# A recurrent attention loop rescheduled: compact softmax factors, shared vector passes, attention moved by transfers

## The reference

```python
Pn = rmsnorm(P, input_norm_w)              # context: 4 x 64 x 256
k_proj = Pn @ Wk.T
v_proj = Pn @ Wv.T
for _ in range(NUM_ITERS):                 # 3
    sn = rmsnorm(slots, slot_norm_w)       # slots: 4 x 1024 x 256
    q_proj = sn @ Wq.T
    scores = jnp.einsum('bkd,bmd->bkm', q_proj, k_proj) * SCALE
    attn = jax.nn.softmax(scores, axis=-2)             # over the 1024 slots
    attn = attn / (jnp.sum(attn, axis=-1, keepdims=True) + EPS)   # over the 64 context rows
    updates = jnp.einsum('bkm,bmd->bkd', attn, v_proj)
    slots = gru_cell(updates, slots, gru_wih, gru_whh, gru_bih, gru_bhh)
...
# gru_cell: r = sigmoid(xr + hr); z = sigmoid(xz + hz); n = tanh(xn + r * hn)
#           new = (1 - z) * n + z * h
...
x = x + tanh(g_xattn) * slots
x = x + tanh(g_ffn) * moe(layernorm(x))    # 16 experts, and a shared one
```

## Time and profile before

| | us |
|---|---|
| median of 3 runs | 1268.45 (1265.12 to 1269.66) |
| profiled execution | 1267.16 |
| its span, first to last instruction | 1265.4 |
| loop, TensorE's first to last unit | 92.9 to 457.6 |
| experts and dense part after it | 462.7 to the end |

### The profile page before, as it was taken

The page is one execution under the profiler, slowest core; times in us unless marked ns, Lnnn a source line. Parts: engine busy times, 40 slices in busy tenths (PEclk is TensorE's granted clock), DMA queues, the critical chain, the costliest instruction groups (busy, mean ns, idle before and its releaser), DMA issues. The chain is left out here.

```text
span 1265.4 us, 18034 instructions
## 1 busy us (share of the span) xinstructions
PE 1140.1 (90%) x6000; PEld 952.3 (75%) x6000; DVE 880.7 (70%) x1618; ACT 567.6 (45%) x834; POOL 414.0 (33%) x319
## 2 busy tenths in 40 slices
PE   5659989898999864799997999999999999999995
PEld 3447767676777654688886888888888888888884
DVE  7586787878788669677894566666666666666652
ACT  4244545454545426423223544545454455454441
POOL 4242333333310024234353143334332343332331
PEclk9659999999999986899998999999999999999998
DMA  4200000000000034400014444444444444444421
GB/s 153 89 9 9 1 17 1 17 0 17 0 17 9 9 118 133 125 17 33 17 34 150 154 118 125 129 134 112 106 125 126 134 134 114 103 129 120 134 35 17
DMA packets 45603, 95.58 MB, mean 76 GB/s; under 512 B 11008, under 2 KB 36864, under 8 KB 41216
## 3 DMA queue, kind: packets, MB, share of 16 engines
q1 hardware_dynamic: 31808, 75.98, 18.1%
q0 software_dynamic: 12288, 17.31, 8.2%
q10 hardware_dynamic: 1472, 1.84, 0.4%
HBM read 74.11 MB, written 17.07 MB: 72 GB/s over the span
## 5 line engine op out<-in xcount | busy, mean ns | idle before, releaser
L1921 DVE SCALAR_TENSOR_TENSOR ehid<-eup,b_up,esilu 128x512 f32<-128x512 f32 x128 | 96.1, 751 | 180.9 <-PE eup L1790 164.7
L1758 POOL DMA_INDIRECT out_tokens<-yo,idx_out x64 | 114.9, 1796 | 240.5 <-DVE yo L1895 225.9
L1844 ACT ACTIVATE esilu<-egate,b_gate 128x512 f32<-128x512 f32 x128 | 87.7, 685 | 156.6 <-PE egate L1790 153.5
L1803 PE MATMUL edown<-w_hi,eh_hi 128*128 128x256 f32 x512 | 145.3, 284 | 0.0
L1803 PE MATMUL edown<-w_hi,eh_lo 128*128 128x256 f32 x512 | 144.3, 282 | 0.0
L1803 PE MATMUL edown<-w_lo,eh_hi 128*128 128x256 f32 x512 | 143.0, 279 | 0.0
L1853 ACT ACTIVATE eh_hi<-ehid 128x512 fp32r<-128x512 f32 x128 | 81.1, 633 | 114.9 <-DVE ehid L1921 114.9
L1873 DVE TENSOR_TENSOR w_lo<-raw,w_hi 128x768 fp32r<-128x768 f32 x128 | 121.2, 949 | 2.0 <-ACT w_hi L1833 2.0
L522 PE MATMUL gate_banks<-slots_hi,whh_hi 128*128 128x512 f32 x288 | 117.4, 408 | 4.6 <-ACT tr L660 4.5
L522 PE MATMUL gate_banks<-slots_hi,whh_lo 128*128 128x512 f32 x288 | 114.7, 398 | 0.0
L522 PE MATMUL gate_banks<-slots_lo,whh_hi 128*128 128x512 f32 x288 | 114.6, 398 | 0.0
(11 more groups left out here) (287 smaller groups left out, 2698.9 us busy)
## 6 DMA issues: line engine op xcount, KB each, us to landing
raw<-in_w_expert SPq DMA_DIRECT2D x32, 1536.0 KB
token_rows<-work SPq DMA_DIRECT2D x8, 512.0 KB, 3.2
out_tokens<-y SPq DMA_DIRECT2D x8, 512.0 KB, 3.0
attn<-attn_lo SPq DMA_DIRECT2D x24, 128.0 KB, 2.3
work<-in_x SPq DMA_DIRECT2D x4, 512.0 KB, 4.8
raw<-in_x SPq DMA_DIRECT2D x4, 512.0 KB, 6.7
b_down<-in_down_b SPq DMA_DIRECT2D x1, 2048.0 KB, 9.2
raw<-in_w_shared SPq DMA_DIRECT2D x1, 1536.0 KB, 11.3
```

The costliest lines, as they stand in the source:

```text
L1758: pool.indirect_dma_start(out, bass.IndirectOffsetOnAxis(idx_out[:, j:j + 1], 0), yo[:, j, :], None, compute_op=ALU.add).then_inc(g_add, 16)
L1803: last = nc.tensor.matmul(edown[:, j // 2, (j % 2) * D:(j % 2 + 1) * D], h[:, f % RING, tok], w[:, f, 4 * P:6 * P], start=(f == 0 and m == ...
L1844: nc.scalar.activation(esilu[:, f % 2, :], egate[:, f % 2, :], ACT.Silu, bias=b_gate[:, bass.ds(e, 1), f:f + 1].rearrange("p a b -> p (a b ...
L1921: nc.vector.scalar_tensor_tensor(ehid[:, f % 2, :], eup[:, f % 2, :], b_up[:, bass.ds(e, 1), f:f + 1].rearrange("p a b -> p (a b)"), esilu ...
```

## The change

It leaves setup's results, the number of matmuls for gates and scores, the dense part and the experts as they are. In the loop:

- **Column sums and their reciprocal in compact form.** `column_sums` makes a 128 x 16 tile (tokens on partitions; eight matmuls with `expo` as the weights and a 128 x 2 `rsum` as the moving operand). VectorE adds epsilon and takes the reciprocal there, and splits it in a high and a low part (`two_parts`, in `rec_parts`). `turn_rec` transposes it, `own_columns` lays it out in `spread`, `spread_rec` spreads it over the partitions into the `score` bank. `copy_csum` and the wide reciprocals are gone. `rms` is split in the same way, and both spreads are fp32r matmuls over 128 rows in place of fp32 ones over 16.
- **Placement.** `turn_rms` stands right behind `scores`; `spread_rms` in and behind unit (1,0); `column_sums` in unit (2,0), `turn_rec` behind it, `spread_rec` in unit (2,1). VectorE does `token_rms` and `spread_steps` ahead of the slot passes of group 0, scaling and `maximum` between the two `pre` of group 1, attention in group 2 and its low part in group 3.
- **Shared vector passes.** The three passes that make new slots run once per group over both chunks (1024 columns) instead of once per unit. `tz` is doubled for this.
- **Attention by transfers.** `attention_hi` writes the high part into `rms_c`, `attention_lo` the low part in place into `expo`, each over 128 rows in one instruction; `move_attention` brings both to `attn` with four transfers for each half instead of two.
- **GpSimd** keeps squares, sums and low parts, now released by group (`v_new`). It has three memsets more at the start of the loop, and four selections more in setup.

```diff
                 def column_sums(s):
 
                     pe.wait_ge(v_rsum, s + 1)
+                    for c in range(2 * BLK):
+                        last = nc.tensor.matmul(csum_t.rearrange("p (b c) -> p b c", b=2)[:, :, c],
+                                                expo[:, c * P:(c + 1) * P], rsum[:, :], start=True, stop=True)
+                    last.then_inc(m_csum, 1)
+
+                def turn_rec(s):
+
+                    pe.wait_ge(v_recd, s + 1)
+                    nc.tensor.transpose(rms_b[:, 0:P], rec_parts[:, :], ident[:, :]).then_inc(m_rect, 1)
+
+                def spread_rec(s):
+
+                    pe.wait_ge(v_dia2, s + 1)
                     for h in range(2):
-                        nc.tensor.matmul(score[:, h, :], rsum[:, :], expo[:, h * GROUP:(h + 1) * GROUP],
-                                         start=True, stop=True).then_inc(m_csum, 1)
+                        nc.tensor.matmul(score[:, h, :], pick_group[:, h, :], spread[:, :, :].rearrange("p b t -> p (b t)"),
+                                         start=True, stop=True).then_inc(m_rec, 1)
...
                         sum_squares(pe, first_run - 1, 1 - pair, GPP - 1, (v_ms, s))
                         scores(s, 1 - pair, first_run - GPP)
-                    gru_unit(it, pair, 1, 0, (lambda: turn_rms(s)) if softmax else None)
-                    if softmax:
-                        spread_rms(s, 0)
-                    gru_unit(it, pair, 1, 1)
+                        turn_rms(s)
+                    gru_unit(it, pair, 1, 0, (lambda: spread_rms(s, 0)) if softmax else None)
                     if softmax:
                         spread_rms(s, 1)
+                    gru_unit(it, pair, 1, 1)
                     if more:
                         sum_squares(pe, first_run, pair, 0, (v_ms, s + 1))
-                    gru_unit(it, pair, 2, 0)
-                    gru_unit(it, pair, 2, 1)
+                    gru_unit(it, pair, 2, 0, (lambda: column_sums(s)) if softmax else None)
                     if softmax:
-                        column_sums(s)
+                        turn_rec(s)
+                    gru_unit(it, pair, 2, 1, (lambda: spread_rec(s)) if softmax else None)
...
-                def move_low(s, pair, h):
-
+                def move_attention(s, pair, h):
+
+                    half = slice(h * GROUP, (h + 1) * GROUP)
                     sp.wait_ge(v_alo, 2 * s + h + 1)
                     for b in range(2):
-                        sp.dma_start(attn[rows_of(1 - b), pair, b, h * GROUP:(h + 1) * GROUP].bitcast(F32),
-                                     attn_lo[rows_of(b), :].bitcast(F32)).then_inc(d_alo, 16)
+                        sp.dma_start(attn[rows_of(b), pair, b, half].bitcast(F32), rms_c[rows_of(b), h, :]).then_inc(d_attn[h], 16)
+                        sp.dma_start(attn[rows_of(1 - b), pair, b, half].bitcast(F32), expo[rows_of(b), half]).then_inc(d_attn[h], 16)
...
+                    gru_unit(it, pair, 0, 0, None, (last_high,) if softmax else ())
+                    gru_unit(it, pair, 0, 1)
+                    if softmax:
+                        gru_unit(it, pair, 1, 0, lambda: copy_rms(s, 0), high(0), (lambda: copy_rms(s, 1),))
+                        gru_unit(it, pair, 1, 1, None, (lambda: exponentials(s),))
                     else:
...
+                        gru_unit(it, pair, 1, 0, None, high(0))
+                        gru_unit(it, pair, 1, 1)
+                    gru_unit(it, pair, 2, 0, None, high(1))
+                    gru_unit(it, pair, 2, 1, None, tuple((lambda h=h: attention_hi(s, h)) for h in range(2)) if softmax else ())
+                    gru_unit(it, pair, 3, 0, None, high(2))
                     gru_unit(it, pair, 3, 1)
...
-                def gru_unit(it, pair, g4, c, meanwhile=None):
-
-
-                    u = it * UNITS + (pair * GPP + g4) * 2 + c
+                def gru_group(it, pair, g4, first=(), second=()):
+
+
+                    g = it * G + pair * GPP + g4
                     sl = tokens(pair, g4)
...
+                    for c, between in enumerate((first, second)):
+                        u = it * UNITS + (pair * GPP + g4) * 2 + c
+                        dve.wait_ge(a_r, u + 2)
+                        dve.wait_ge(a_h, u + 2)
+                        nc.vector.scalar_tensor_tensor(pre[:, :], tr[:, c, :], 1.0, hb[:, c, :], ALU.add,
+                                                       ALU.mult).then_inc(v_q, 1)
+                        dve.wait_ge(v_q, u + 3)
+                        dve.wait_ge(m_x, u + 1)
+                        nc.vector.tensor_tensor(pre[:, :], pre[:, :], gate_x[:, :], ALU.add).then_inc(v_pre, 1)
+                        for step in between:
+                            step()
                     dve.wait_ge(a_n, u + 1)
-                    nc.vector.tensor_tensor(dif[:, :], slots[:, c, sl], nn[:, c, :], ALU.subtract).then_inc(v_dif, 1)
-                    dve.wait_ge(v_dif, u + 1)
+                    nc.vector.tensor_tensor(dif[:, :, :], slots[:, :, sl], nn[:, :, :], ALU.subtract).then_inc(v_mix, 1)
+                    dve.wait_ge(v_mix, 2 * g + 1)
                     dve.wait_ge(a_z, u + 2)
...
+                def two_parts(parts, full, v_high, count, v_done):
+
+                    high, low = parts[:, 0:NB].bitcast(F32R), parts[:, LOW:NR].bitcast(F32R)
+                    nc.vector.tensor_copy(high, full[:, :]).then_inc(v_high, 1)
+                    dve.wait_ge(v_high, count)
+                    nc.vector.tensor_tensor(low, full[:, :], parts[:, 0:NB], ALU.subtract).then_inc(v_done, 1)
...
+                def csum_reciprocal(s):
+
+                    dve.wait_ge(m_csum, s + 1)
+                    nc.vector.tensor_scalar(csum_e[:, :], csum_t, ATTN_EPS, None, ALU.add).then_inc(v_rec, 1)
+                    dve.wait_ge(v_rec, 3 * s + 1)
+                    nc.vector.reciprocal(rec[:, :], csum_e[:, :]).then_inc(v_rec, 1)
+                    dve.wait_ge(v_rec, 3 * s + 2)
+                    two_parts(rec_parts, rec, v_rec, 3 * (s + 1), v_recd)
...
+                    gru_group(it, pair, 0, (), (lambda: token_rms(s, 1 - pair), lambda: spread_steps(s)))
+                    gru_group(it, pair, 1, (lambda: scale_scores(s, 0), lambda: scale_scores(s, 1), lambda: maximum(s)),
+                              (lambda: token_sum(s),))
+                    csum_reciprocal(s)
+                    gru_group(it, pair, 2, (lambda: spread_reciprocal(s), lambda: attention_half(s, 0),
+                                            lambda: attention_half(s, 1)))
+                    gru_group(it, pair, 3, (lambda: attention_lo(s, 0), lambda: attention_lo(s, 1)))
```

More of the change, by code:

```diff
@@ L451, in flamingo_kernel @@
             v_q = sem("v_q")
-            v_pre, v_dif, v_mix, v_new = (sem(f"v_{n}") for n in ("pre", "dif", "mix", "new"))
+            v_pre, v_mix, v_new = (sem(f"v_{n}") for n in ("pre", "mix", "new"))
             v_ms = sem("v_ms")
@@ L561, in gru_unit, with scores @@
                     from_attention(gate_x, 4 + c, True).then_inc(m_x, 1)
-                def scores(s, pair, split_before):
+                def scores(s, pair, split_before, first=False):
+                    if not first:
+                        pe.wait_ge(v_attn, 2 * s)
                     for h in range(2):
@@ L635, in _ @@
                 sum_squares(pe, G1 - 1, 0, G1 - 1)
-                scores(0, 0, 0)
+                scores(0, 0, 0, True)
                 turn_rms(0)
@@ L640, in _ @@
                 column_sums(0)
+                turn_rec(0)
+                spread_rec(0)
                 for g in range(G1, G):
@@ L667, in gru_unit, with copy_rms @@
                                          scale=0.5).then_inc(a_h, 1)
-                    if meanwhile is not None:
-                        meanwhile()
+                    for step in meanwhile:
+                        step()
                     act.wait_ge(v_pre, u + 2)
                     nc.scalar.activation(nn[:, c, :], pre[:, :], ACT.Tanh, bias=b_xn[:, c:c + 1]).then_inc(a_n, 1)
+                    for step in after:
+                        step()
                 def slots_high(it, pair, g4):
-                    act.wait_ge(v_new, it * UNITS + (pair * GPP + g4) * 2 + 3)
+                    act.wait_ge(v_new, it * G + pair * GPP + g4 + 2)
                     sl = tokens(pair, g4)
                     nc.scalar.activation(slots_hi[:, :, sl], slots[:, :, sl], ACT.Copy).then_inc(s_hi, 1)
-                def copy_rms(s, h):
+                def copy_rms(s, h, first=False):
                     act.wait_ge(m_rms, 2 * s + h + 1)
+                    if not first:
+                        act.wait_ge(d_attn[h], DMA_ATTN * s)
                     nc.scalar.activation(rms_c[:, h, :], rms_b[:, :], ACT.Copy).then_inc(a_rms, 1)
@@ L701, in half_iteration, with high @@
                 def half_iteration(it, pair, softmax, more=True):
                     s = 2 * it + pair + 1
```

(29 more changed lines are left out.)

213 lines of the change are left out of this document (93 added, 120 removed).

## The result

The changed kernel takes 1234.03 us, the median of 4 runs (1232.23 to 1235.07), beside 1266.78 us (1263.93 to 1269.66) for the kernel before on the same chip: a ratio of 0.974, with a 95% interval of 0.9712 to 0.9768. That is 32.8 us faster. The forecast was 1238 with a range of 1232 to 1256. The profiled execution of the changed kernel took 1234.22.

What follows compares the result with a forecast made beforehand. TensorE was taken to bound the loop, plus four waits per half from VectorE's order. Gains of 17.2 + 3.8 + 3.3 + 6.0 + 1.1 less 1.9 made 29.5: 1267.2 - 29.5 = 1237.7, forecast 1238 us, range 1232 to 1256.

Steps and rivals of the forecast that it cites:

- The five waits: TensorE's waits in the old loop: attention landing, `rms`, `pre`, `rsum`, and one in the last half; 24.0 us.
- the walk: Step-by-step timing of one changed half iteration from TensorE's first matmul; it put the next half's begin at 57.4 us.
- TensorE's own work: Matmul time per half: cheaper `rms` spreads less added transposes and spreads, 0.85 us less, bounds 0.4 and 1.4.
- Waits that went: Four steady TensorE waits per regular half vanish: 4.9 us, plus 0.15 restart for each of four.
- Waits that came: New TensorE waits charged per regular half, 0.3 us at `turn_rec` and 0.3 for the attention's transfers: 0.6.
- the landing: Arrival of the attention's low part for the next half: old wait 1.7 us gone, 0.7 in hand, worst 1.1 late.
- rival (1): Waits come back at `turn_rec`, attention transfers and `rms`, 3.2 us a half: 1248; chance 0.21 with slow transfers.
- 5.5 + 0.85 - 0.6 = 5.75: Gain per regular half in us: vanished waits with restarts, plus less matmul work, minus new waits; 17.2 for three.
- The loop's start: Before the loop, `normalise` starts 1.1 us earlier without the column-sum copies; setup loses 0.3.
- The tail: Behind TensorE's last matmul, the last group's three passes are exposed at double width: 1.6 us lost.
- Rival (3): The lock between VectorE and GpSimd makes VectorE the bound, a half 67.9 us: slower, 1275; chance 0.08.
- Rival (2): The recurrence sets the pace, TensorE waiting at the sum of squares 7.0 us a half: no gain, 1264; chance 0.07.

Runs made afterwards that it cites:

- experiment 1: GpSimd's loop squares, sums and low parts cut to 16 columns: in the kernel before 1242.96 us, in the changed kernel 1230.61 us.
- experiment 2: The kernel before with each reciprocal piece over 16 columns instead of 256: 1257.03 us, ratio 0.9934.
- experiment 6: The changed kernel with both low parts of the attention moved behind both `pre` of group 3: 1243.83 us, ratio 0.9807.
- Experiment 8: The changed kernel with TensorE's list at the end of setup reordered, group 4's first transpose ahead of the column sums' spread: 1229.01 us, ratio 0.9715.
- experiment 4: The changed kernel with the four spreading matmuls of a half as fp32 instead of fp32r: 1247.0 us, ratio 0.9844.
- experiment 5: The changed kernel with `token_rms` and `spread_steps` put back behind the slot passes of group 0: 1274.08 us, ratio 1.0049.
- experiment 3: The changed kernel with the three slot passes run per unit over 512 columns again, as before: 1236.41 us, ratio 0.9754.

## Why the prediction was right

**The mechanism and the place of the time** are as walked. The five waits are gone; the walk has `rec_parts` ready at 37.95 of a half and the trace at 38.0 (189.81 - 151.80), `rms_parts` ready at 16.2 and the trace at 16.8, so TensorE has 0.9 us in hand there, where 1.5 were walked. VectorE's timeline of the changed kernel in the second half shows both, and what the walk forecast for the reciprocals:

```profile
168.44 0.18 DVE L845 TENSOR_TENSOR rms_parts<-rms,rms_parts 128x16 fp32r<-128x16 f32 x1
...
187.61 0.17 DVE L884 TENSOR_SCALAR csum_e<-rms_b 128x16 f32<-128x16 f32 x1
187.82 0.25 DVE L886 RECIPROCAL rec<-csum_e 128x16 f32<-128x16 f32 x1
188.11 1.50 DVE L843 CAST rec_parts<-rec 128x16 fp32r<-128x16 f32 x1
189.64 0.17 DVE L845 TENSOR_TENSOR rec_parts<-rec,rec_parts 128x16 fp32r<-128x16 f32 x1
189.89 1.64 DVE L805 SCALAR_TENSOR_TENSOR pre<-tr,hb 128x512 f32<-128x512 f32 x1
```

The copy of the high part stands 1.50 us, under GpSimd's square, and TensorE meets it:

```profile
187.68 1.89 POOL L962 TENSOR_TENSOR square<-slots 128x1024 f32<-128x1024 f32 x1 [7.52 <-DVE slots L819]
...
189.87 0.33 PE L623 MATMUL rms_b<-ident,rec_parts 128*128 128x128 f32 x1 [0.34 <-DVE rec_parts L845]
```

Four VectorE reciprocals of 1.7 us in each half have become one of 0.25.

**TensorE's own work: the term that was too small.** 0.85 was forecast for a half and 1.5 is measured (experiment 1), just outside the bounds of 0.4 to 1.4. First, the prediction's terms were added wrongly: 1.64 - 0.14 - 0.1 - 0.46 is 0.94. The rest can be read from two halves without waits, one with each order (the second halves of experiment 1's two kernels). Every matmul counts from its start to the next one's:

| | before | after | saved | forecast |
|---|---|---|---|---|
| two spreads of `rms` | 2.10 | 0.47 | 1.64 | 1.64 |
| two `spread_rec` | | 0.47 | -0.47 | -0.46 |
| transposes | 0.03 | 0.05 | -0.03 | -0.24 |
| column sums | 1.72 | 1.70 | 0.01 | 0 |
| gate matmuls | 45.28 | 45.00 | 0.28 | 0 |
| sums of squares | 3.34 | 3.24 | 0.10 | 0 |
| scores | 5.53 | 5.56 | -0.03 | 0 |
| half | 58.00 | 56.49 | 1.51 | 0.94 |

Two terms were mis-sized: the transposes cost next to nothing, and the gate matmuls, which the prediction held to be unchanged, lose the gaps beside the fp32 spreads. TensorE's timeline of the kernel before, first half, shows one spread and its neighbours:

```profile
120.62 0.39 PE L531 MATMUL gate_banks<-attn,vw_lo 128*128 128x512 f32 x1
120.94 1.12 PE L589 MATMUL rms_b<-spread,pick_group 16*128 16x512 f32 x2
121.99 0.50 PE L522 MATMUL gate_banks<-slots_hi,whh_hi 128*128 128x512 f32 x1
122.32 0.39 PE L522 MATMUL gate_banks<-slots_lo,whh_hi 128*128 128x512 f32 x1
```

It starts 0.32 behind the matmul ahead of it, and the first two matmuls behind it are 0.33 apart, instead of 0.23. The same places in the changed kernel:

```profile
169.47 0.27 PE L601 MATMUL rms_b<-ident,rms_parts 128*128 128x128 f32 x1
...
173.28 0.39 PE L609 MATMUL rms_b<-spread,pick_group 128*128 128x512 f32 x1
173.51 0.39 PE L541 MATMUL gate_banks<-slots_hi,whh_hi 128*128 128x512 f32 x1
...
185.73 1.84 PE L616 MATMUL rms_b<-rsum,expo 128*128 128x2 f32 x16
187.43 0.48 PE L541 MATMUL gate_banks<-slots_hi,whh_hi 128*128 128x512 f32 x1
```

**Waits that went.** Forecast 4.9 + 0.6 for restarts; 63.9 - 58.0 = 5.9 measured. The split was off: the four waits are 1.8, 1.7, 0.6 and 0.6 in the trace, 4.7, so 1.2 stands behind them, 0.3 each and not 0.15. VectorE's order and GpSimd's holding of it were rightly the cause. The prediction named four reciprocals, the half-height pieces and blocked passes without weighing them; experiment 2 takes 2.2 of a half away by the reciprocals alone, experiment 1 all 5.9 by GpSimd alone, so the two are not to be added.

**Waits that came.** 0.6 charged, 0.6 found, but in another split: all at `turn_rec`, none at the landing, where 0.7 us in hand were walked and 2.1 are there. The four issues take up to 0.60 each one behind the other and the last lands 2.4 us on, so all is there some 4.2 after the first issue; the estimate of 4.0 was near, the low part was only earlier than walked. So rival (1) did not come; experiment 6 shows what such a wait costs, 1.9 a half.

**5.5 + 0.85 - 0.6 = 5.75 against 5.9 + 1.5 - 0.6 = 6.8.** That difference of 1.1 by the half iterations, with 0.9 in the first half and 1.3 in the fifth, is why the loop gained 5.8 us beyond the forecast. Two of the three terms around it took 2.6 back:

- The loop's start gained nothing, where 0.8 was forecast. `normalise` did start at 71.33 instead of 72.51, but then ScalarE waited 0.98 for the first transposes, which stand behind the column sums' spread in TensorE's list, and GpSimd's last sum took 2.12, beside a VectorE `slots_lo` of 2.79. The step that failed is the one that stopped at ScalarE's start: what was next late stands one engine further on. Experiment 8 undoes it, 3.9 us. A single trace is a weak witness for 0.8, though: the loop starts between 91.5 and 93.3 in the six kernels that have the changed kernel's setup, and at 91.4, 92.1 and 92.9 in the three that have the setup of before.
- The tail lost 1.5, as forecast (1.6).
- Behind the loop 1.7 us were lost that the prediction put at nothing. In the changed kernel the first loads of `x` in the dense part are awaited for 5.55 us after their issue, before for 3.57:

```profile
428.14 0.94 SPq L1129 DMA_DIRECT2D work<-in_x  x2
433.69 1.41 DVE L1491 SCALAR_TENSOR_TENSOR slots<-down,tanh_g,work 128x512 f32<-128x512 f32 x2 [5.85 <-DMA work<-in_x]
```

The code of these loads is the same. Of the kernels run, the kernel before, the two made from it (experiments 1 and 2) and experiment 4 have 3.5 to 3.6, the changed kernel and all others made from it 5.3 to 5.8. Experiment 4 is the changed kernel but for a data type, so it isn't the change as such; what sets it stays open.

**The rivals that would have changed the sign.** Rival (3): VectorE is held as the prediction described, but its busy time, holds included, is 43.4 of 57.1 us, and its lateness shows in 0.6 a half. What the holds come to is 7.7 us a half: 43.36 against 35.6 in the changed kernel with small GpSimd work, where the prediction walked 37.8 of undisturbed work and the rival took all of GpSimd's 23.1. Before the change they were 9.6 (53.15 against 43.6). The Trainium skill's page "SBUF — State Buffer", section "SBUF: two separate sides", says that a VectorE operation in a mode that uses two ports, or one with two SBUF inputs where the GpSimd operation reads SBUF too, and a GpSimd operation exclude each other. The trace agrees for two inputs: L805 took 1.64 instead of 0.69. The copy L843 and, in experiment 5, the integer step L41, with one input each, took 1.50 and 1.88 instead of 0.17; in which mode they ran no run shows. Not every step is held: the reciprocal L886 took its 0.25 inside the same GpSimd square, and a pass with one input in PSUM its usual 0.69 beside a GpSimd instruction (L809). Rival (2), waiting for squares, has no row in the loop. What would have brought a result on the slower side is neither: it is `token_rms` left in its old place while TensorE asks for `rms` right behind `scores` (experiment 5), which the prediction did not weigh, since the change moves both at once.

## What to carry to other kernels

A short chain of small VectorE steps that TensorE waits for belongs ahead of the pass that releases GpSimd, never behind it: the same 14 steps cost nothing ahead of the slot passes and 8 us a half behind them. Whoever moves the consumer of a result to an earlier place has to move its producer too. Count TensorE's own work from a stretch without waits, made by an experiment if need be, and with the gaps on both sides of what is replaced; and follow every gain ahead of a loop to the engine that is late next. And when passes are shared to save instructions, keep them split where they are the last thing on the path.

## What the runs showed of the hardware

- A VectorE step on 128 x 16 takes 0.17 us, and up to 1.9 when a GpSimd pass has begun ahead of it: in experiment 5 the held steps L41 and L44 end within 0.04 us of GpSimd's two instructions. The reciprocal of a 128 x 16 tile was not held (0.25).
- After an idle stretch of 6.07 us TensorE ran eight matmuls of 512 columns 0.43 apart instead of 0.23. The length of the wait just ahead doesn't settle it: such a stretch also came behind 1.25 us (experiment 3, third half), 2.1 (experiment 2, last half) and 2.78 (the changed kernel, start of the loop), and once with no wait within 8 us ahead (experiment 2, at 314.57, fourth half), while the regular halves of the kernel before, with waits of up to 1.9 us, have a granted clock of 1.00.
- An fp32 matmul of 512 columns with 16 rows costs 1.05 from its start to the next, and 0.1 more in each gap to a neighbouring gate matmul; an fp32r one with 128 rows 0.23.
- Transfers issued by SyncE: 0.46 us the first and 0.60 each further one, one behind the other, and the last one's data at most 2.4 us after its issue began.
- The same two loads took 3.5 to 3.6 or 5.3 to 5.8 us from issue to use, depending on the kernel, with no cause found.
